# Moving the turning of the one-hots ahead of a barrier, cutting the range look-ups in four, and issuing the stores from ScalarE

## The reference, cut to what matters

```
xf = layernorm(y) * gamma + beta                  # y: output of the first block
tile_idx = the best of 64 tiles for each token, by signs
x_slice  = the 16 channels of xf that belong to the tile
mn, mx   = min and max of x_slice over ALL tokens of the same tile
u = clip((x_slice - mn) / (mx - mn + 1e-8), 0, 1 - 1e-6);  gi = int(u * 16)
delta = (bases[tile, j, gi] + slopes[tile, j, gi] * x_local) * scale[tile]
z = y with delta added to those 16 channels;  out = layernorm(y + z)
```

## Time and profile before

| what | value |
|---|---|
| median of 3 runs | 1338.6 us (1338.29 to 1341.18) |
| the profiled execution: its own time | 1339.66 us |
| its span (first to last instruction) | 1337.9 us |
| busy share of the span | PE 86%, DVE 79%, ACT 71%, POOL 62% |
| end of the barrier between the two parts | 1135.8 us |
| transfers of 2 MB issued in the second part | 12 loads (units 3 to 14) and 16 stores |

### The profile page before, as it was taken

One profiled execution on the slowest core, in us unless ns is written; L12 is line 12 of the kernel. 1 busy time (PEld: TensorE's weight loads), 2 busy tenths in 40 slices (PEclk: granted clock), 3 DMA queues, 4 the chain that ended last, 5 costly groups with the idle time before them and its releaser, 6 DMA issues. The chain is left out here.

```text
span 1337.9 us, 31770 instructions
## 1 busy us (share of the span) xinstructions
PE 1155.3 (86%) x9346; PEld 733.8 (55%) x9346; DVE 1056.9 (79%) x2490; ACT 950.9 (71%) x1809; POOL 833.0 (62%) x1692
## 2 busy tenths in 40 slices
PE   5799999999999999999999999999999761769300
PEld 4556666666666666666666666666666331521000
DVE  4898988898999998899999999999998846278400
ACT  4668888888888888888888888888887542326740
POOL 3125676767676767676767676767676645015755
PEclk8899999999999999999999999999999875555555
DMA  4013333222333222222222222222221126828995
GB/s 138 33 56 112 113 115 107 99 99 99 102 111 113 104 102 101 100 99 99 99 99 99 99 99 99 99 99 99 99 99 69 69 98 227 350 90 309 408 413 204
DMA packets 64066, 175.05 MB, mean 131 GB/s; under 512 B 11531, under 2 KB 23059, under 8 KB 64022
## 3 DMA queue, kind: packets, MB, share of 16 engines
q1 hardware_dynamic: 57878, 172.40, 34.5%
q0 software_dynamic: 6144, 2.11, 1.1%
HBM read 69.06 MB, written 101.20 MB: 127 GB/s over the span
## 5 line engine op out<-in xcount | busy, mean ns | idle before, releaser
L1010 DVE SCALAR_TENSOR_TENSOR acc<-xT_all,cw_sb,acc 128x256 f32<-128x256 f32 x768 | 353.9, 519 | 6.8 <-ACT acc L714 6.8
L740 ACT ACTIVATE sg<-TX,bet,gam 128x256 f16<-128x256 f32 x256 | 129.6, 556 | 40.4 <-PE TX L437 40.3
L457 PE MATMUL PR<-xT_all,w_sb 128*128 128x256 f32 x512 | 137.3, 392 | 3.3 <-ACT xT_all L678 3.3
L1342 POOL TENSOR_TENSOR AT<-AT,Wm 128x128 f32<-128x128 f32 x224 | 114.7, 512 | 40.4 <-DVE AT L1036 24.6
L469 PE MATMUL WK<-w_sb,tS 128*128 128x512 f32 x256 | 137.4, 618 | 0.0
L714 ACT ACTIVATE acc<-xT_all,cb_sb,cw_sb 128x256 f32<-128x256 f32 x256 | 132.5, 591 | 4.4 <-DVE xT_all L996 2.5
L511 PE MATMUL OB<-th_all,AT 128*128 128x512 f32 x256 | 124.6, 609 | 12.1 <-POOL AT L1342 10.6
L539 PE MATMUL PR<-shT,w_mg_sb 128*64 128x128 f32 x2048 | 128.8, 280 | 6.4 <-ACT shT L723 6.4
L539 PE MATMUL PR<-shT,w_rk_sb 128*64 128x128 f32 x2048 | 125.9, 276 | 0.0
L539 PEld LDWEIGHTS PR<-shT,w_rk_sb 128*64 128x64 f32 x2048 | 110.5, 137 | 25.8 <-issue 25.8
L539 PEld LDWEIGHTS PR<-shT,w_mg_sb 128*64 128x64 f32 x2048 | 113.4, 139 | 18.8 <-issue 12.1
(11 more groups left out here) (226 smaller groups left out, 2658.9 us busy)
## 6 DMA issues: line engine op xcount, KB each, us to landing
xin_all<-in_x SPq DMA_DIRECT2D x32, 1024.0 KB
y_ring<-y_all SPq DMA_DIRECT2D x32, 1024.0 KB, 4.1
y_scratch<-y_all SPq DMA_DIRECT2D x32, 1024.0 KB, 6.1
own<-y_scratch SPq DMA_DIRECT2D x9, 2048.0 KB, 24.5
out<-own SPq DMA_DIRECT2D x9, 2048.0 KB, 24.0
RX<-RE SPq DMA_DIRECT2D x128, 32.2 KB
xT_all<-y_scratch SPq DMA_DIRECT2D x2, 2048.0 KB, 13.0
th_all<-y_scratch SPq DMA_DIRECT2D x2, 2048.0 KB, 14.5
```

What stands on the lines that cost most here:

```text
L457: i = pe.matmul(PR[:, 0:T], w0_sb[:, blk, :], xT[b][:, blk, HIST:HIST + T], start=(blk == 0), stop=(blk == NB - 1))
L740: nc.scalar.activation(sg[:, blk, :], TX[:, (blk % 2) * T:(blk % 2 + 1) * T], ACT.Sign, scale=gam[:, blk:blk + 1], bias=bet[:, blk:blk + 1 ...
L1010: v.scalar_tensor_tensor(acc[:, blk, :], xT[b][:, blk, i:i + T], cw_sb[:, blk, i:i + 1], acc[:, blk, :], ALU.mult, ALU.add).then_inc(e_con ...
L1342: q.tensor_tensor(late, late, Wm[:, :, l, :].rearrange("p c (n h) -> p c n h", h=h), ALU.add)\
```

## The change

- **Ahead of the barrier.** After its pipeline TensorE turns the first seven eights of one-hots, into two PSUM tiles `OT` that lie where `PR` and `SC0` were, and ScalarE copies them to `ohT`. `extremes` raises a semaphore `s_oh` when its part of `oh` is there. `ident_bf` is made at the start of the first part. The last eight (chunks 56 to 63) are turned in the second part, into a tile `OT2`; that copy stands in ScalarE's program behind the rows of batch 0.
- **Ranges in four pieces**, chunks 0 to 3, 4 to 11, 12 to 35 and 36 to 63, each just ahead of the first batch that needs it, on TensorE and VectorE alike. `OT2` and the ranges' tile keep their two PSUM banks, so there are three tiles Z in place of four.
- **Five row buffers are loaded ahead of the barrier** (PRE = 5, OWN = 3). Two new ones lie over memory that the first part no longer needs. Units 0 and 1 are loaded by `first_rows`, between SyncE's last `spread` and its last `store`; units 2, 3 and 4 after that store.
- **Stores from ScalarE.** ScalarE waits for its own fourth row of a unit and issues the store on its own queue; those of unit 15 go row by row. SyncE issues loads alone.
- **Scatters** are spread by a list: after `moments(k)`, k = 0 to 6, GpSimd has done the units below 0, 1, 3, 4, 6, 9, 16.

The core of the diff:

```diff
-    PRE, OWN = 3, 5
+    PRE, OWN = 5, 3
+    EXT_ENDS = (16, 40, 56, 64)
 # SyncE, first part, in its step
+                def first_rows():
+                    done(sp, e_proj, NG - 1)
+                    done(sp, e_t, NG - 1)
+                    done(sp, e_res[1], NG - 1)
+                    for b in range(2):
+                        sp.wait_ge(d_yst[b], (NG - 2) * 16)
+                    sp.dma_start(slots[0], y_u[0]).then_inc(r_ld[0], 16)
+                    sp.dma_start(slots[1], y_u[1]).then_inc(r_ld[1], 16)
                     if live(g, 3):
                         spread(*of(3))
+                    if isinstance(g, int) and g - 3 == NG - 1:
+                        first_rows()
                     if live(g, 3):
                         store(*of(3))
 # TensorE, end of the first part
+                for f in range(NC // 8 - 1):
+                    pe.wait_ge(s_oh, 2 + [f * 8 < end for end in EXT_ENDS].index(True))
+                    if f >= 2:
+                        pe.wait_ge(s_ohe, f - 1)
+                    for j in range(8):
+                        for rows in (slice(0, NT), slice(NT, P)):
+                            i = pe.transpose(OT[f % 2][rows, j, :], oh[:, :, f * 8 + j], ident_bf[:])
+                    i.then_inc(s_oht, 1)
 # ScalarE, end of the first part
+                for f in range(NC // 8 - 1):
+                    act.wait_ge(s_oht, f + 1)
+                    nc.scalar.activation(ohT[:, f * 8:(f + 1) * 8, :], OT[f % 2][:], ACT.Copy).then_inc(s_ohe, 1)
 # second part
+            RANGES = ((0, 4), (4, 12), (12, 36), (36, NC))
 # SyncE
-                for u in range(U):
-                    sp.wait_ge(p_row, 4 * (u + 1))
-                    sp.dma_start(out_u[u], slot(u)).then_inc(p_st[slot_id(u)], 16)
-                    old = u - 2
-                    if 0 <= old and old + NS < U - 1:
-                        sp.wait_ge(p_st[slot_id(old)], stored(old))
-                        load(old + NS)
+                for u in range(NS, U - 1):
+                    sp.wait_ge(p_st[slot_id(u)], stored(u - NS))
+                    load(u)
 # GpSimd
+                BEHIND = (0, 1, 3, 4, 6, 9, U)
                 for k in range(len(BATCHES)):
                     moments(k)
-                    while 4 * (behind + 1) <= starts[max(k - 1, 0)]:
-                        scatter(behind)
-                        behind += 1
+                    for u in range(BEHIND[k - 1] if k else 0, BEHIND[k]):
+                        scatter(u)
 # TensorE
-                    if s >= 4:
-                        pe.wait_ge(p_zf, s - 3)
+                    if s >= 3:
+                        pe.wait_ge(p_zf, s - 2)
+                ranges(*RANGES[0])
+                tables(0)
+                tables(1)
+                ranges(*RANGES[1])
+                last_turned()
+                for s in range(2, 6):
+                    tables(s)
+                ranges(*RANGES[2])
+                for s in range(6, 12):
+                    tables(s)
+                ranges(*RANGES[3])
+                for s in range(12, PAIRS):
+                    tables(s)
 # ScalarE
-                for f in range(NC // 8):
-                    act.wait_ge(p_ohT, f + 1)
-                    nc.scalar.activation(ohT[:, f * 8:(f + 1) * 8, :], OT[:], ACT.Copy).then_inc(p_ohTe, 1)
+                        if u == U - 1:
+                            act.wait_ge(p_row, n + 1)
+                            nc.scalar.dma_start(out_u[u, :, n % 4, :], row).then_inc(p_sl[n % 4], 16)
+                        elif n % 4 == 3:
+                            act.wait_ge(p_row, n + 1)
+                            nc.scalar.dma_start(out_u[u], slot(u)).then_inc(p_st[slot_id(u)], 16)
+                    if k == 0:
+                        act.wait_ge(p_ohT, 1)
+                        nc.scalar.activation(ohT[:, NC - 8:NC, :], OT2[:], ACT.Copy).then_inc(p_ohTe, 1)
 # VectorE
+                ready = 0
+                for k in range(len(BATCHES)):
+                    if starts[k] == RANGES[ready][0]:
+                        ranges_in(*RANGES[ready])
+                        dve.wait_ge(p_rc, ready + 1)
+                        cells(*RANGES[ready])
+                        ready = min(ready + 1, len(RANGES) - 1)
                     batch(k)
-                    corrections(k - 1)
+                    if k:
+                        corrections(k - 1)
```

More of the change, by code:

```diff
@@ L106, in build @@
         y_all = sbw("y_all", [P, 2, CPG, D])
+        ident_bf = sbw("ident_bf", [P, P], BF16)
+        with ExitStack() as loop_only:
+            acc = loop_only.enter_context(nc.sbuf_tensor("acc", [P, NB, T], F32))
+            shT = loop_only.enter_context(nc.sbuf_tensor("shT", [P, NB, T], F32))
+        rows1 = sbw("rows1", [P, 4, D])
+        with ExitStack() as loop_only:
+            X = loop_only.enter_context(nc.sbuf_tensor("X", [P, KSLOTS, CH], F32))
+            E = loop_only.enter_context(nc.sbuf_tensor("E", [P, SLOTS, CH], F32))
+            RE = loop_only.enter_context(nc.sbuf_tensor("RE", [P, RSLOTS, RPITCH], F32))
+            KE = loop_only.enter_context(nc.sbuf_tensor("KE", [P, KSLOTS, CH], F32))
+        rows2 = sbw("rows2", [P, (2 * KSLOTS + SLOTS) * CH + RSLOTS * RPITCH])
+        with ExitStack() as loop_only:
+            w_rk_sb = loop_only.enter_context(nc.sbuf_tensor("w_rk_sb", [P, NB, P], F32))
+            w_mg_sb = loop_only.enter_context(nc.sbuf_tensor("w_mg_sb", [P, NB, P], F32))
+            w0_sb = loop_only.enter_context(nc.sbuf_tensor("w0_sb", [P, NB, R], F32))
+            w1_sb = loop_only.enter_context(nc.sbuf_tensor("w1_sb", [P, D], F32))
+        ohT = sbw("ohT", [P, NC, P], BF16)
+        slots = [xT_all[:].rearrange("p i b t -> p (i b t)")[:, 0:4 * D].rearrange("p (n d) -> p n d", n=4), rows1[:],
+                 rows2[:, 0:4 * D].rearrange("p (n d) -> p n d", n=4), th_all[:],
+                 zT_all[:].rearrange("p i b t -> p (i b t)").rearrange("p (n d) -> p n d", n=4)]
         r_ld = [whole.enter_context(nc.semaphore(f"r_ld{i}")) for i in range(SLOTS4)]
@@ L217, in build @@
             TX = psum("TX", [P, HALF])
-            PR = psum("PR", [P, HALF])
-            SC = [psum(f"SC{i}", [P, HALF]) for i in range(CPG)]
+            with ExitStack() as loop_only:
+                PR = loop_only.enter_context(nc.psum_tensor("PR", [P, HALF], F32))
+                SC0 = loop_only.enter_context(nc.psum_tensor("SC0", [P, HALF], F32))
+            OT = [psum(f"OT{i}", [P, 8, P], BF16) for i in range(2)]
+            SC = [SC0, psum("SC1", [P, HALF])]
             WK = [psum(f"WK{i}", [P, HALF]) for i in range(2)]
@@ L242, in build @@
             s_pc = sem("s_pc")
+            s_oh = sem("s_oh")
+            s_oht = sem("s_oht")
+            s_ohe = sem("s_ohe")
             d_xin = [sem(f"d_xin{i}") for i in range(2)]
@@ L402, in _ @@
                 pipeline(sp, step, 3, NG // 2 - 1)
[L403 to L409, removed]
+                done(sp, e_A, NG - 1)
+                done(sp, e_keT, NG - 1)
+                done(sp, e_dec, NG - 1)
+                sp.wait_ge(d_rx, NG * 64)
+                sp.dma_start(slots[2], y_u[2]).then_inc(r_ld[2], 16)
                 done(sp, e_o[1], NG - 1)
                 done(sp, e_su[1], NG - 1)
-                sp.dma_start(th_all[:], y_u[1]).then_inc(r_ld[1], 16)
-                sp.dma_start(zT_all[:].rearrange("p i b t -> p (i b t)").rearrange("p (n d) -> p n d", n=4), y_u[2])\
-                    .then_inc(r_ld[2], 16)
+                sp.dma_start(slots[3], y_u[3]).then_inc(r_ld[3], 16)
+                sp.dma_start(slots[4], y_u[4]).then_inc(r_ld[4], 16)
                 for b in range(2):
@@ L660, in _ @@
                 pipeline(pe, step, 4)
+                for e in (e_xs, e_kk, e_ks, e_rr, e_at0[0]):
+                    done(pe, e, NG - 1)
+                for f in range(NC // 8 - 1):
[6 more added lines that the diff above has]
+                    i.then_inc(s_oht, 1)
             @block.scalar
@@ L969, in spline_tables @@
                     link(v.tensor_copy(t2s2[:], t2i[0:NT, :]))
+                    v.tensor_copy(ident_bf[:], ident[:]).then_inc(s_oh, 1)
                 def extremes(lo, hi):
@@ L1513, in build @@
             p_sum, p_m, p_coef, p_row, p_out, p_sc, p_i = (sem(n) for n in ("p_sum", "p_m", "p_coef", "p_row", "p_out", "p_sc", "p_i"))
[L1514 to L1518, removed]
+            p_st = [sem(f"p_st{i}") for i in range(SLOTS4 - 1)]
+            p_sl = [sem(f"p_sl{i}") for i in range(4)]
+            slots.extend(o[:] for o in own)
             last_slot = y_all[:].rearrange("p i c d -> p (i c) d")
@@ L1608, in _, with last_turned @@
             def _(pe):
-                def turned(f):
-                    if f:
-                        pe.wait_ge(p_ohTe, f)
+                def last_turned():
+                    f = NC // 8 - 1
                     for j in range(8):
                         for rows in (slice(0, NT), slice(NT, P)):
```

(10 more changed lines are left out.)

72 lines of the change are left out of this document (17 added, 55 removed).

## The result

The changed kernel takes 1309.6 us (median of 4 runs, 1308.8 to 1311.3), the old one in the same rounds 1338.8: ratio 0.978, 95% interval 0.976 to 0.980, 29.2 us less. Forecast were 1307.1, and 1292 to 1318.

The account below looks back on a forecast made before the run. Transfers were taken to bound the old kernel; earlier rows would move the end to GpSimd's scatters, from 1331.0 to 1299.5. 1339.66 - 31.5 = 1308.1, or 1307.1 against the median; range 1292 to 1318.

Parts of the forecast that it names:

- What bounds the old kernel: End of the old kernel: transfers set it, the DMA engines being full from 1220.35 us at 413 GB/s.
- early rows are the lever: Second part: DMA engines often idle before 1220.35 us because no row is finished; the question is how early rows come.
- Up to the barrier no change: First part, to the barrier at 1135.84: effect taken as 0; a gather's wait of 4.55 us could come once more.
- The chain in the second part: Behind the barrier: first rows of batches 1 to 3 at 1166.4, 1188.0, 1207.9; sums of batch 4 at 1225.5.
- The price of the lost tile Z: VectorE with three tiles Z: a batch of twelve takes 14.8 us, 1.8 to 2.3 more than before.
- The end is GpSimd's: End of the kernel: scatters come last at 1299.5, while unit 15's store lands at 1287.
- The size: Whole kernel: end 31.5 us earlier, 1308.1 against the profiled execution, 1307.1 against the median.
- Preloads at nothing: Loads ahead of the barrier: units 0 and 1 over by 1094, units 2 to 4 replacing three loads; effect taken as 0.
- Stores from ScalarE: Second part: ScalarE issues each store itself, about 0.4 us an issue, the first store at 1156.
- The count of 5.53 us a unit: DMA engines: 5.53 us per 2 MB unit with its share of scatters; 17 units from 1192.9 take 94 us.
- The rival of the clock: TensorE in the second part: clock rises from 1.2 to 2.4 GHz, VectorE never waits for a pair; 1290 us, chance 0.08.
- The stall on ScalarE's issues: ScalarE's store issues take up to 7.64 us each between units of rows; 1366 us, slower than before, chance 0.05.

Follow-up runs that it names:

- k6: Changed kernel with ranges and cells in two pieces (chunks 0 to 3 and 4 to 63) in place of four: 1331.7 us.
- k7: Changed kernel with all one-hots turned in the second part again, ranges still in four pieces: 1324.7 us.
- k11: Changed kernel with both undone: all one-hots turned in the second part, and ranges in two pieces: 1335.2 us.
- k1: Changed kernel measured again without any edit: 1308.4 us, ratio 0.977 to the old kernel.
- k9: Changed kernel without the 24 scatters of units 9 to 14: 1294.1 us.
- k3: Changed kernel with three units loaded ahead of the barrier in place of five; units 3 and 4 loaded behind it: 1308.6 us.
- k4: Changed kernel with stores issued by SyncE again, in the old order with the loads: 1312.9 us.
- k2: Changed kernel with the scatter list altered to 0, 1, 3, 6, 8, 11, 16, so more are done earlier: 1304.4 us.

## Why the prediction was right, by its steps

- **What bounds the old kernel, and that early rows are the lever**: right. That its end is set by transfers was read from its trace, and no run changes the old kernel by that alone. That early rows are the lever is shown: k6 and k7 take the two means away and lose 21 and 16 of 31 us, and k11 shows that together they carry 27.
- **Up to the barrier no change**: right by k1 (1135.38). The seven copies end at 1132.40, 6.1 us ahead of the barrier of that execution, and no gather came later than in the old kernel (the wait for one is 4.44 us, 4.55 in the earlier trace rows).
- **The chain in the second part**, counted from the barrier's end, forecast and measured: first rows of batch 0 at 15.2 and 15.4 us, of batch 1 at 30.6 and 29.5, of batch 2 at 52.2 and 52.2, of batch 3 at 72.1 and 72.6; sums of batch 4 at 89.7 and 89.7; first of the 28 scatters at 128.4 and 128.7; end of the last at 163.7 and 163.8. The price of the lost tile Z was in it: a batch of twelve was to take 14.8 us on VectorE, and batch 5 takes 14.9 (1228.70 to 1243.61), where the old kernel took 12.9 to 13.1. No run gives the fourth tile back, so the price rests on these rows.
- **The end is GpSimd's**: right, shown by k9. The transfers were to end at 151 us from the barrier. The last store is issued at 1274.03 and takes at least 15.4 us to land, so it lands at 1289.4, 150.9 us from the barrier, 12 us ahead of the last scatter.
- **The size.** I forecast 31.5 us for the profiled execution, and the stretch is shorter by 31.4. The times differ by 29.2 and 31.0 in two measurements. The old kernel's second trace gives 194.0 for its stretch, hence 30.2, so that 31.5 and 31.4 agree so closely is in part luck. The two profiled executions differ by 28.3 in time, since the changed one's barrier came 2.7 us later. Subtracting 1.06 us for the old kernel's execution was finer than that noise.
- **Preloads at nothing**: right by k3. **Stores from ScalarE**: I named no gain for them beside the order of work, and they carry about 4 us (k4). It didn't hurt the forecast, since the sum went straight to the changed order, in which no scatter waits. The count of 5.53 us a unit held for single units too: store 9 was to land at 1254, 118 us from the barrier, and landed at 1256.0, 117.5 from its own. By the same count store 7 is the ninth transfer from 1192.9 on and lands at 1242.7. The scatters of unit 7 came behind that in the changed kernel's list; in k2's they didn't, and waited until 1240.94. What failed there was k2's expectation, which left this count out.
- **The rival of the clock** didn't come: the granted clock is 0.50 through the second part, in 1180 to 1190 with TensorE busy 10.00 of 10 us. It was above 0.50 for some 7 us, but ahead of the barrier (last section), where nothing of the end hangs on TensorE. The stall on ScalarE's issues is real (k6) and did not come here.

## What to carry to other kernels

When a stage is bound by transfers that begin late, ask first what makes the first piece late, and then which in-order queue ends last once the transfers are hidden: here it was GpSimd, 11 to 13 us behind them. A wait in the middle of an in-order program costs all that is queued behind it, so place such work where its input has surely landed and not where the engine is first free. Two parts of a change that feed the same wait must be judged together: undone singly they cost 21 and 16 us, together 27.

## What the runs showed of the hardware

The granted clock of TensorE was 0.50 in the old kernel from 1110 us to the end. In the changed one it is 0.57 in 1120 to 1130 and 0.77 in 1130 to 1140, around 112 small transposes between 1122.87 and 1131.34, and 0.50 again from 1140 on. In slices of 2 us it is 0.50 up to 1128, then 0.86, twice 1.00, 0.85, and 0.50 from 1136 on: so for some 7 us it was at 2.4 GHz, and it was back at 1.2 GHz ahead of the barrier's end. In k7 and k11, without these transposes, it stays at 0.50 there. Of the nine traces with them it rose in seven; in k2 and k3 it stayed at 0.50. The rise gave back nothing that can be measured: sixteen transposes take 1.16 to 1.22 us at 1.00 (k1) and 1.20 to 1.25 at 0.50.

Yet in the old kernel, from 1210 to 1240, TensorE is busy 10.00 us in each 10 with table matmuls and stays at 1.2 GHz. The Trainium skill ("TensorE: Matmul & The Clock Gate", Part 1) has activity release the gate; the seven rises behind the transposes agree with it, while k2, k3 and the table and range matmuls don't. Why was not tried.
